# Order of the token preparation in an attention with positions by node: products and sums one turn earlier, rotation first, weighted sum one unit behind

## The reference

```python
q, k, v, logits = x @ Wq, x @ Wk, x @ Wv, x @ Wr          # logits: 4 nodes for each head
node_probs = softmax(logits)                               # over the 4 nodes
pos = clip(cumsum(node_probs, tokens) - node_probs, 0, 2047)
cos, sin = tables at pos, linear between whole positions   # for each node
cos_w, sin_w = sum over nodes of node_probs * cos, * sin
q_r = q * cos_w + rotate_half(q) * sin_w                   # k_r likewise
scores = q_r @ k_r.T * scale + log(node_probs @ node_probs.T + 1e-8)
out = softmax(causal(scores)) @ v ; x = x + out @ Wo
```

## Time and profile before

| what | value |
|---|---|
| time, median of 3 runs | 3235.47 us (3217.61 to 3240.35) |
| the profiled execution's own time | 3241.71 us, its span 3240.0 us |
| TensorE busy | 2571.2 us (79%) |
| VectorE busy | 1837.3 us (57%) |
| ScalarE busy | 1656.2 us (51%) |
| GpSimd busy | 569.0 us (18%) |
| lead turns | from about 484 to 763 us |
| main loop | from 778 to about 2740 us |

### The profile page before, as it was taken

How to read it: one execution, slowest core, us unless ns; L and a number is a source line. 1 busy time by engine, 2 the same in 40 slices (tenths; PEclk the granted TensorE clock), 3 DMA queues, 4 the chain that set the end, 5 groups by cost and what they waited for, 6 DMA issues and landing times. The chain is left out here.

```text
span 3240.0 us, 108362 instructions
## 1 busy us (share of the span) xinstructions
PE 2571.2 (79%) x48340; PEld 2086.0 (64%) x48342; DVE 1837.3 (57%) x3767; ACT 1656.2 (51%) x2032; POOL 569.0 (18%) x525
## 2 busy tenths in 40 slices
PE   8028835555999999999999999999999999831785
PEld 8015512224878877787787788778899987730553
DVE  6874317886657656665666566665422222678441
ACT  2002213444777777677776777777666665200221
POOL 0126860001110100000000000000000000010687
PEclk6559876667999999999999999999999999555887
DMA  7204540111111111111111211121111111610355
GB/s 246 81 27 83 96 63 19 39 37 36 51 45 43 47 47 49 42 58 52 55 43 44 62 53 47 42 64 43 53 45 48 44 44 47 206 42 0 84 99 68
DMA packets 180105, 194.13 MB, mean 60 GB/s; under 512 B 30992, under 2 KB 163104, under 8 KB 179488
## 3 DMA queue, kind: packets, MB, share of 16 engines
q1 hardware_dynamic: 155040, 152.75, 15.7%
q0 software_dynamic: 24576, 34.10, 6.7%
HBM read 119.10 MB, written 76.02 MB: 60 GB/s over the span
## 5 line engine op out<-in xcount | busy, mean ns | idle before, releaser
L1072 ACT ACTIVATE at_ew<-at_ring 128x1024 f32<-128x1024 f32 (+2 forms) x1280 | 1127.2, 897 | 413.4 <-PE at_ring L1450 238.4
L1471 PEld LDWEIGHTS at_mix<-at_val,at_ew 128*64 128x64 f32 x34816 | 1222.6, 137 | 139.3 <-issue 6.1
L1471 PE MATMUL at_mix<-at_val,at_ew 128*64 128x68 f32 x34816 | 1265.4, 223 | 4.0 <-issue 3.5
L1450 PE MATMUL at_ring<-at_qT,at_kT 98*64 98x512 bf16 (+3 forms) x5120 | 739.2, 350 | 39.0 <-ACT at_ew L1072 20.5
L1319 DVE TENSOR_TENSOR at_mixed<-at_mix,at_prob 128x272 f32<-128x272 f32 x256 | 112.2, 438 | 774.0 <-PE at_mix L1471 773.2
L1450 PEld LDWEIGHTS at_ring<-at_qT,at_kT 98*64 98x64 bf16 x5120 | 272.6, 111 | 113.1 <-issue 47.1
L331 ACT ACTIVATE ffn_w1T<-ffn_pair 128x512 f32<-128x512 f32 x16 | 9.6, 598 | 482.7 <-PE ffn_pair L657 460.8
L1017 POOL TENSOR_TENSOR at_val<-at_prob,at_eps_t 128x64 f32<-128x64 f32 x64 | 20.9, 327 | 1330.7 <-PE at_mix L1471 1330.7
L1523 PE MATMUL at_side<-at_w_all,at_turned 128*64 128x512 f32 (+1 forms) x1024 | 210.8, 559 | 18.4 <-ACT at_turned L1081 10.6
L283 POOL DMA_INDIRECT out_dram<-ffn_y,ffn_idx_all x128 | 212.8, 1663 | 47.8 <-issue 37.8
L1454 PE MATMUL at_ring<-at_late_kq,at_ident_b 128*64 128x128 bf16 x2048 | 209.1, 220 | 0.8 <-issue 0.7
(11 more groups left out here) (212 smaller groups left out, 3224.8 us busy)
## 6 DMA issues: line engine op xcount, KB each, us to landing
table<-ffn_xn SPq DMA_DIRECT2D x32, 512.0 KB, 3.4
q_parts<-at_parts SPq DMA_DIRECT2D x64, 192.0 KB, 2.5
k_parts<-at_parts SPq DMA_DIRECT2D x64, 192.0 KB, 2.8
at_qT<-q_parts SPq DMA_DIRECT2D x64, 192.0 KB
at_kT<-k_parts SPq DMA_DIRECT2D x64, 192.0 KB
ffn_xin<-in_L_attn_x_dram SPq DMA_DIRECT2D x16, 512.0 KB, 5.6
ffn_w_in<-in_L_ffn_w_dram SPq DMA_DIRECT2D x32, 256.0 KB, 3.7
at_xin<-out_dram SPq DMA_DIRECT2D x32, 256.0 KB, 3.1
```

The source lines that it names most:

```text
L1072: act.activation(ew[u % NE_BUF][:, 0:w], ring[u % 2][:, 0:w], ACT.Exp).then_inc(s["exp_ready"], 1)
L1450: lastm = pe.matmul(ring[u % 2][h:h + HALF, at:at + w], kT[q][:, (j + n) * P + h:(j + n) * P + h + HALF], qT[q][:, c * 512 + t * P:(c + 1) ...
L1471: lastm = pe.matmul(mix[c % 2][h:h + HALF, t * K * VW:(t + 1) * K * VW], ew[u % NE_BUF][:, col + h:col + h + HALF], val[q][:, j + n, :, :] ...
```

## The change

On VectorE `node_products` and `node_sums` of a pair move from the turn in which it is `fin` to the end of the turn in which it is `new`. `turn_weights` and `rotate` then stand at the head of the next turn, ahead of `shift_logits`, `node_softmax` and `positions`. In the main loop the steps between the calls of `mix_nodes` are dealt out anew. On TensorE and ScalarE most side steps come earlier by three slots; `sums_before` stays in slot 11. The weighted sum of a unit comes one slot later, and `ew` has five tiles for four.

```diff
-        NE_BUF = 4
+        NE_BUF = 5
...
-                    side_steps = {4: copy_turned, 6: copy_v_logits, 9: copy_outputs, 10: softmax_exp, 19: high_part,
-                                  21: square, 22: middle_part, 25: low_part, 32: trig, 34: copy_qk, 36: next_rsqrt}
+                    side_steps = {4: copy_turned, 6: copy_v_logits, 9: softmax_exp, 10: copy_outputs, 15: square, 16: high_part,
+                                  18: middle_part, 21: low_part, 29: trig, 31: copy_qk, 33: next_rsqrt}
...
                     if ip is None:
                         if fin is not None:
-                            node_products(fin)
-                            node_sums()
+                            turn_weights()
+                            rotate(fin)
                         shift_logits(new)
-                        if fin is not None:
-                            turn_weights()
                         node_softmax(new)
-                        if fin is not None:
-                            rotate(fin)
                         positions(new)
                         statistics(new + 1)
                         angles(new)
@@
                             largest_squares(fin)
                             bound(fin)
+                        node_products(new)
+                        node_sums()
                         return
```

```diff
-                    side_steps = {1: turn_inputs, 3: project_values, 6: turn_outputs, 9: output, 11: sums_before, 16: turn_rotated,
-                                  18: take_high_off, 21: take_middle_off, 26: turn_squares, 29: project_qk}
+                    side_steps = {1: turn_inputs, 3: project_values, 7: turn_outputs, 9: output, 11: sums_before, 13: turn_rotated,
+                                  15: take_high_off, 18: take_middle_off, 22: turn_squares, 26: project_qk}
                     for u in range(2 * NU):
...
-                        weighted(head, u % NU)
+                        if at > 0:
+                            weighted((at - 1) // NU, (at - 1) % NU)
                         if u in side_steps:
                             side_steps[u]()
+                    if 2 * ip + 2 == HEADS:
+                        weighted(HEADS - 1, NU - 1)
```

More of the change, by code:

```diff
@@ L1390, in run @@
                     if fin is not None:
-                        node_products(fin)
+                        turn_weights()
+                        rotate(fin)
+                    if new is not None:
+                        shift_logits(new)
                     mix_nodes(i, 1)
                     if new is not None:
[L1394 to L1397, removed]
                         node_softmax(new)
[L1399 to L1404, removed]
                         positions(new)
@@ L1407, in run @@
                         add_residual(post, 0, 1)
+                    mix_nodes(i, 2)
+                    if new is not None:
+                        angles(new)
+                    if fin is not None:
+                        largest_squares(fin)
                     find_maxima(i + 1)
                     mix_nodes(i, 3)
-                    if new is not None:
-                        angles(new)
+                    if more:
+                        statistics(new + 1)
                     mix_nodes(i + 1, 0)
                     if fin is not None:
-                        largest_squares(fin)
+                        bound(fin)
                     mix_nodes(i + 1, 1)
[L1416 to L1419, removed]
                     mix_nodes(i + 1, 2)
+                    if new is not None:
+                        node_products(new)
                     if more:
                         normalise(new + 1)
+                    if new is not None:
+                        node_sums()
                     if i + 2 < HEADS:
@@ L1626, in run @@
                         return
-                    side_steps = {1: turn_inputs, 3: project_values, 6: turn_outputs, 9: output, 11: sums_before, 16: turn_rotated,
-                                  18: take_high_off, 21: take_middle_off, 26: turn_squares, 29: project_qk}
-                    i = 2 * ip
+                    side_steps = {1: turn_inputs, 3: project_values, 7: turn_outputs, 9: output, 11: sums_before, 13: turn_rotated,
+                                  15: take_high_off, 18: take_middle_off, 22: turn_squares, 26: project_qk}
                     for u in range(2 * NU):
[L1632 to L1638, removed]
-                        weighted(head, u % NU)
+                        at = ip * 2 * NU + u
+                        if at + 2 < HEADS * NU:
+                            if (at + 2) % NU == 0:
+                                begin_head((at + 2) // NU)
+                            scores((at + 2) // NU, (at + 2) % NU)
+                        if at > 0:
+                            weighted((at - 1) // NU, (at - 1) % NU)
                         if u in side_steps:
                             side_steps[u]()
+                    if 2 * ip + 2 == HEADS:
+                        weighted(HEADS - 1, NU - 1)
                 def project_output(q, at):
```

2 lines of the change are left out of this document (added).

## The result

| | before | changed |
|---|---|---|
| median | 3227.76 us (3217.61 to 3240.35, 4 runs) | 3297.89 us (3290.22 to 3303.89, 4 runs) |
| profiled execution's own time | 3241.71 us | 3294.70 us |

The ratio is 1.0214, 95% interval 1.0165 to 1.0264: slower by some 70 us, and by 53 us between the two profiled executions, which are the ones that can be compared stage by stage. The forecast was 3269, the range up to 3295.

A forecast was written before the change was run, and what follows sets the result against it. The main loop was taken as bound by TensorE's work plus waits, the lead turns by a chain through VectorE, TensorE and ScalarE. 19 + 2 - 3.3 + 9 + 13 - 5.9 = +33.8 gave a median of 3269 us, range 3240 to 3295.

The forecast's parts named there:

- Lead turns, +19: Turns before the main loop: running sum and exponential no longer hidden under `rotate`, 2.6 us in each of eight; +19 us.
- The 1.8 us of the last lead turn: Last lead turn: a `rotate` operation no longer slowed while GpSimd makes the first values, 0.69 instead of 2.50 us; -1.8.
- Residual wait, +2 and -3.3: TensorE at `turn_rotated`: residual-sum wait stays, 1.98 for 1.85 us in 15 turns, +2; `positions` wait without `post` goes, -3.3.
- the squares' wait: TensorE at `turn_squares`: `largest_squares` ends some 7 us ahead, so the wait goes; -5.9 us.
- Sines, +9: Main loop, slot 29: wait for the exponential after the sines grows from 0.84 to 1.22 us in 23 turns; +9 us.
- Slot 9, +13: Main loop: VectorE's chain to `shift_logits` delays unit 9's exponential, 0.4 us with `post`, 1.0 without; +13 us.
- The clock, chance 0.03: Rival: TensorE's clock falls in the longer waits, 2 us in each of 23 turns, +46, giving 3315; chance 0.03.
- +14.8 forecast for the main loop: Main-loop terms: residual wait +2, `positions` wait -3.3, sines +9, slot 9 +13, squares -5.9.
- The lag itself adds no matmul ... All of these at 0: Small main-loop effects: lag, fifth `ew`, GpSimd's values and SyncE's stores, each priced at 0.

The follow-up runs named there:

- e2: Changed kernel with the lead turns in the order of the kernel before; 3272 us, ratio 1.0142 to the kernel before.
- e10: Changed kernel with `shift_logits` moved ahead of `rotate` in the main loop, nothing else; 3268 us, ratio 1.0141 to the kernel before.
- e1: Changed kernel with VectorE adding the residual sum ahead of `positions`; 3240 us, ratio 1.0037 to the kernel before.
- e9: Changed kernel with the lag undone: weighted sum of the same unit, four tiles of exponentials; 3222 us, ratio 0.9993 to the kernel before.
- e5: Kernel before with two unused VectorE copies added ahead of the residual sum in 15 turns, lengthening its wait; 3257 us, ratio 1.0074.
- e3: Changed kernel with `project_qk` and the sine steps back in their old slots, lag kept; 3267 us, ratio 1.0121 to the kernel before.
- e8: Changed kernel with residual sum ahead of `positions`, old lead turns, sines in old slots, `shift_logits` ahead of `rotate`; 3186 us, ratio 0.9855 to the kernel before.
- e6: Kernel before with the lag alone: weighted sum one unit behind, five tiles of exponentials; 3344 us, ratio 1.0357.
- e7: Kernel before with the residual sum ahead of `rotate` and `positions`, plus the lag; 3272 us, ratio 1.0129.

## Why the prediction was wrong

- **The way was right, the size wrong:** +34 forecast, +70 measured by the medians (+53 between the profiled executions), beyond the range's 3295.
- **Lead turns, +19:** right in place and size. 16.6 us between the profiled executions (309.6 against 293.0), 21.5 by undoing it in e2, 20 between the means of all runs of either order. The 1.8 us of the last lead turn came back as said.
- **Residual wait, +2 and -3.3:** right as a wait. I had 1.98 us as the view counts it; it is 1.97 (29.7 for 27.7 us in all). The wait for `positions` and the squares' wait went as said.
- **Sines, +9:** right: I had 1.22 us, it is 1.19.
- **Slot 9, +13:** the place was right, the size too small: 19.6 us in 23 turns, 0.6 each instead of 0.4 with `post`, 1.3 instead of 1.0 without. Taken away in e10, with the falls of the clock that went too, it was worth 24 to 30 us.
- **The clock, chance 0.03: this is the step that failed.** I set "the main loop's time" to "TensorE's work, which the change leaves as it is, plus TensorE's waits", so the sum has no term for the same work taking longer. The waits come out near the forecast: +14.8 forecast for the main loop, 17.9 measured over the 22 turns. What is missing is the 19.6 us more of busy time. I wrote that 0.99 with waits of up to 2.3 us spoke against it. The one wait of 2.3 us of the kernel before (2.27) was in fact followed by a long `turn_rotated` (3.26 us, at 1768), and that turn lies in the very stretch of the earlier trace rows; all others were 1.8, and the mean clock hid the one. Between the two kernels the residual wait went from 1.82 to 1.97 us and the turns with a fall from 0 of 14 (1 of 15 with the longer wait) to 12 of 15; 12 x 1.6 = 19 us. e1, e9 and e5 show that the residual wait brings the falls: with it taken away or at 1.38 us there are none, and lengthened they come in the kernel before too.
- **"The lag itself adds no matmul ... All of these at 0": failed too,** though its effects stood in other terms of my sum without its name. It took the full sums out of slots 12 and 26, where TensorE's work covers a wait (I computed with the short ones, and took no notice that it's the lag that puts them there), and made each group of `mix_nodes` one slot later for VectorE, which is the slot 9 wait. e9: without the lag the whole change comes out level with the kernel before, though its slower lead turns are still there.

Added up from the changed kernel by the medians: residual wait and clock 57 us, lead 26, shift 30 (e10), sines 30 (e3), 143 in all. e8 with all four is faster by some 116 us, by the ratios. So they overlap: both e3 and e10 shorten the slot 9 waits, and the single runs had fewer falls of the clock, which can go only once.

What stays open: why equal waits of 1.97 us are followed by a fall in 12, 8, 8 and 6 of 15 turns (changed kernel, e2, e3, e10). e2 differs from the changed kernel in nothing but the lead turns, so the other waits of the turn aren't enough to explain it; and each count comes from one profiled execution. And of the 70 us by the medians, 17 lie outside what the two profiled executions show: the one before was 14 us slower than its median, the one after 3 us faster.

## What to carry to other kernels

A software pipeline's lag isn't free because it adds no work: it moves every hand-over to the engine behind, and it changes which short or long piece covers each wait. Where the loop alternates uneven pieces, count the cover for each wait anew. When a wait of the bound engine is found, ask first whether the step it waits for can stand somewhere else in the releasing engine's list: one addition moved past steps it doesn't depend on was worth 31 to 37 us here. And where the same work takes longer after a change, look at the bound engine's clock in short stretches behind its waits: a mean of 0.99 over 300 us can hold a fall.

## What was not expected of the hardware

TensorE's clock can fall after a wait of about 2 us in an otherwise full loop, and the price is nearly as large as the wait: in the turn shown 1.6 us after 1.98. In the changed kernel each of the 12 falls came after the wait, with TensorE at work again; only in e5 (once) and e6 (four times) did one begin within the wait. By wait ahead of `turn_rotated`: 1.38 us, 0 of 15 turns (e9); 1.80 to 1.83, 0 of 14 (before); 1.94 to 2.14, 12, 8, 8 and 6 of 15 (changed, e2, e3, e10); 2.35, 7 of 14, and 2.80 in the one left (e5); 3.8, 12 of 15 (e6). Ahead of the squares, at 1.69 us, it was 2 of 23 both in e6 and in e7. These rows show no sharp limit: 1.69 us is now and then enough, and 3.8 us not always. Ahead of each wait TensorE was at the upper level, 2.4 GHz, but the waits don't stand in the same slot: between the running sum and `turn_rotated` there are five full sums in the kernel before and in e5, and in the changed kernel a short and a full one. The Trainium skill, "TensorE: Matmul & The Clock Gate", section "HAM oscillation — how this bites in real kernels", tells of such re-throttling after waits for a transfer; the waits here are for VectorE and shorter than the page's, and the rows above decide. Here the loss shows as busy time, not as idle time, and so in no list of waits.
